# Six granules instead of nine read part of their channels before the last stores of the first stage

## The chip, the cores and the metric

The kernel runs on one core of a Trainium2 chip. The metric is the device time of one execution in microseconds (us); of several executions the median is given. The profile comes from one more execution, which has a time of its own.

## What is computed

The input x is (16, 128, 64, 64) in float32: 16 images, 128 channels, 64 rows, 64 columns. The reference, cut to what matters:

```
def _gn(v, G=32, eps=1e-05):            # normalise over 4 channels x 64 x 64
    ...
x = x + _L0_conv_ref(_gn(x), L0_conv_weight)       # depthwise 5x5, padding 2
x = x + _L1_conv_ref(_gn(x), L1_conv_rota_matrix)  # einsum('hvc,bchw->bvhw', R, feats)
```

The second part mixes all 128 channels of a pixel with a matrix that depends on the row h. It can begin only when all 128 channels of the first sum (x1 below) and the statistics of all 32 channel groups are known.

## The kernel before, in words

**First stage.** The 32 groups of 4 channels are taken one after the other. A group is 1 MB: 128 partitions (2 halves of 8 images, times 64 rows), with 4 channels, 8 images and 64 columns in each. Its loads come from x in pieces of 256 bytes. TensorE does the convolution as matmuls over the rows (line 661), ScalarE and VectorE add the input (lines 426, 543, 546), and `store` (lines 243 to 247) writes the group to a scratch tensor in DRAM, `x1_dram`, laid out channel first. Groups 0 to 25 are stored from ScalarE's queue, groups 26 to 31 (`SYNC_STORES = 26`) from SyncE's queue (SP). The last group is stored in two halves of two channels, 512 KB each. The statistics of x1 are measured as the groups go by; those of the last 8 groups are picked by a small matmul (line 726) and kept by VectorE (line 616), after which the second stage may normalise.

**Second stage.** x1 is read back with the channels on the partitions. A granule is 4 rows of 8 images: 128 channels with 2048 floats each, 1 MB, in runs of 8 KB. There are 32 granules (`GRANULES`) and 11 buffers for them (`IRING`). ScalarE and GpSimd normalise a granule (lines 471 and 394; VectorE helps with the first, line 622), TensorE multiplies each of its rows with that row's matrix (line 771, preceded by the transposed matrices of line 720), VectorE adds x1 (line 632), and each pair of granules is stored to `out` as one DMA of 2 MB (line 309). The results of a pair stand in one of three buffers (`ORING = 3`).

**The order on SP's queue.** SP issues, in the order of its program, the loads of the first stage, the stores of groups 26 to 31, and everything of the second stage. The change touches what stands between these stores. In the step of the first stage with number 29 (`AHEAD_STEP`), when 28 groups are safely in DRAM (`AHEAD_GROUPS`), SP begins to load the first 112 channels of some granules ahead of the stores of groups 28 to 31 (`load_granule`, lines 274 to 278). When the last store has landed, the remaining 16 channels of each of them follow, 128 KB each; below they are called the tails. Then come the granules that were not begun, whole. The few lines that say this:

```
for n in AHEAD.get(s, ()):
    load_granule(n, slice(0, AHEAD_GROUPS * GC))
...
store(sp, GROUPS - 1, slice(0, 2))
store(sp, GROUPS - 1, slice(2, GC))
groups_stored(sp, GROUPS)
for n in range(EARLY):
    load_granule(n, slice(AHEAD_GROUPS * GC, C))
...
for n in range(EARLY, IRING):
    load_granule(n, slice(0, C))
```

The granules from number 11 on are each loaded when granule n - 11 has been added (SP waits for `out_ready`), and SP's wait for a granule's end stands before the store of its pair and before the next load.

Of the kernel before, what the change touches and what calls it, by code (L numbers as in the profile page):

```python
# [54 lines left out]
SLOT_ORDER = (7, 8, 9, 10, 4, 5, 6, 0, 1, 2, 3)  # L55
AHEAD_GROUPS = 28
AHEAD_STEP = AHEAD_GROUPS + 1
AHEAD = {AHEAD_STEP: range(0, 5), AHEAD_STEP + 1: range(5, 7), AHEAD_STEP + 2: range(7, 9)}
EARLY = 9
SYNC_STORES = 26  # L60
ORING = 3
TURNED = 4
# [9 lines left out]
def conv_rotate_kernel(nc, x, weight, rota, out):  # L72
# [4 lines left out]
    with ExitStack() as ctx:  # L77
# [137 lines left out]
        def granule_landings(n):  # L215
            return 16 * (n // IRING + 1) + (16 if n % IRING < EARLY else 0)

# [31 lines left out]
        def groups_stored(queue, groups):  # L249
            for k in range(YRING):  # L250
                queue.wait_ge(x1_stored[k], 16 * len(range(k, groups, YRING))
                              + (16 if groups == GROUPS and k == (GROUPS - 1) % YRING else 0))
# [7 lines left out]
        def _(sp):  # L260
# [13 lines left out]
            def load_granule(n, channels):  # L274
                u, half = unit_half(n)
                sp.dma_start(tin[n % IRING][channels].rearrange("p h j w -> p (h j w)"),
                             x1_dram[channels, half, u * RH:(u + 1) * RH].rearrange("c h j w -> c (h j w)")
                             ).then_inc(in_landed[n % IRING], 16)

            for s in range(GROUPS + 1):  # L280
# [12 lines left out]
                if s == AHEAD_STEP:  # L293
                    sp.wait_ge(norm2_stored, 32 * (LAST // NBATCH))
                    sp.dma_start(norm2[0:LAST * GC], norm2_dram[0:LAST * GC]).then_inc(norm2_landed, 16)
                    groups_stored(sp, AHEAD_GROUPS)
                for n in AHEAD.get(s, ()):
                    load_granule(n, slice(0, AHEAD_GROUPS * GC))
# [3 lines left out]
# [3 lines that stand above are left out]
# [8 lines left out]

            for n in range(EARLY, IRING):
                load_granule(n, slice(0, C))
# [484 lines left out]
```

## Time and profile before

| | |
|---|---|
| median of 3 runs | 476.41 us (476.32 to 477.0) |
| time of the profiled execution | 472.46 us |
| its span | 470.7 us |
| TensorE busy (matmul) | 414.4 us, 88% |
| VectorE, ScalarE, GpSimd busy | 359.1 us (76%), 275.4 us (59%), 232.1 us (49%) |
| moved by DMA | 139.03 MB, mean 295 GB/s |
| chain that ended last, TensorE and DMA | 65% and 24% of the span |

Times in the trace count from the start of the span. In rows of the timeline the first number is the start, the second the time until the last of the merged instructions ended; a DMA issue is the time of the instruction on the queue, not that of the transfer. The time from an issue to the landing of its data is told by the DMA view alone.

### The profile page before, as it was taken

The page shows a single profiled execution, that of the slowest core. Times are in us where ns is not written, and L with a number is a line of the kernel's source. Part 1 is how long each engine was busy: PE and PEld are TensorE (multiplying, and loading weights), DVE is VectorE, ACT ScalarE, POOL GpSimd, SP SyncE. Part 2 cuts the span into 40 slices and gives each one's busy share as a digit, 9 for nine tenths or more (in the row PEclk, how much of TensorE's full clock was granted, in tenths as well). Part 3 has the DMA queues.
Part 4 walks back from the last instruction along what each step waited for, and adds up shares of the span by engine and source line. Part 5 has one row for each costly group of instructions (what it writes and reads, how often), then busy time and mean ns, then how long its engine had stood idle before and what let it go on. Part 6 is the DMA issues. An engine that isn't in the chain of part 4 may idle for free.

```text
span 470.7 us, 8916 instructions
## 1 busy us (share of the span) xinstructions
PE 414.4 (88%) x3235; PEld 219.6 (47%) x3235; DVE 359.1 (76%) x726; ACT 275.4 (59%) x538; POOL 232.1 (49%) x300
## 2 busy tenths in 40 slices
PE   5888999999999999999999999717999977787791
PEld 5444455555555555555555555413444433333340
DVE  6679999999999999998999975815776544445581
ACT  4164757676675675675676766305777655474560
POOL 5456667665675675665766651003444432242330
PEclk9799999999999999999999999857999999899997
DMA  9989999999989999999999289979999999999997
GB/s 175 198 190 242 262 247 263 260 225 241 318 227 310 259 270 286 241 299 278 251 263 256 110 268 325 313 255 158 416 418 414 411 414 414 419 419 415 407 408 268
DMA packets 177139, 139.03 MB, mean 295 GB/s; under 512 B 137160, under 2 KB 139208, under 8 KB 173000
## 3 DMA queue, kind: packets, MB, share of 16 engines
q1 hardware_dynamic: 159000, 110.15, 80.4%
q10 hardware_dynamic: 18096, 28.32, 17.7%
q8 instruction: 26, 0.43, 0.4%
q14 instruction: 17, 0.14, 0.1%
HBM read 71.32 MB, written 67.12 MB: 294 GB/s over the span
## 4 chain that ended last, share of the span: by engine, by line
PE 65%; DMA 24%; DVE 7%; issue 1%; ACT 1%; ACTq 0%; SPq 0%; DVEq 0%
PE ps L661 55%; DMA out_dram<-area 19%; PE ps L771 8%; DMA x_scratch<-area 3%; DVE area L632 2%; DVE stats L554 2%; DMA area<-in_x_dram 1%; DMA area<-x_scratch 1%; DVE area L546 1%; DVE stats L561 1%; DVE dev L601 1%; PE ps L679 0%; PE ps L671 0%; DVE area L622 0%; ACT area L449 0%
## 5 line engine op out<-in xcount | busy, mean ns | idle before, releaser
L661 PE MATMUL ps<-area 64*64 64x496 f32 (+2 forms) x2560 | 280.6, 589 | 4.2 <-ACT area L449 1.7
L661 PEld LDWEIGHTS ps<-area 64*64 64x64 f32 x2560 | 144.7, 134 | 94.8 <-issue 93.3
L352 POOL TENSOR_TENSOR area<-mask,area 128x325 f32<-128x325 f32 x128 | 130.9, 1046 | 68.5 <-PE ps L661 47.4
L771 PE MATMUL ps<-area 128*128 128x512 f32 x256 | 117.7, 609 | 30.2 <-DVE area L632 17.7
L632 DVE TENSOR_TENSOR area<-ps,area 128x512 f32<-128x512 f32 x128 | 82.2, 686 | 57.9 <-DMA out_dram<-area 39.9
L471 ACT ACTIVATE area<-area,norm 128x256 f32<-128x256 f32 x157 | 80.6, 588 | 61.1 <-PE ps L771 49.8
L449 ACT ACTIVATE area<-area,affine 128x256 f32<-128x256 f32 x189 | 96.4, 588 | 30.1 <-DVE affine L578 30.1
L394 POOL TENSOR_SCALAR area<-area,norm 128x256 f32<-128x256 f32 x95 | 51.7, 557 | 116.8 <-PE ps L771 84.6
L426 ACT ACTIVATE area<-ps 64x512 f32<-64x512 f32 x128 | 75.7, 592 | 47.4 <-PE ps L661 44.9
L771 PEld LDWEIGHTS ps<-area 128*128 128x128 f32 x256 | 48.0, 195 | 89.1 <-issue 56.3
L554 DVE BATCH_NORM_STATS2 stats<-area 128x6 f32<-128x512 f32 x128 | 80.4, 692 | 4.2 <-DMA area<-in_x_dram 4.2
L561 DVE BATCH_NORM_STATS2 stats<-area 128x6 f32<-128x512 f32 x128 | 80.9, 695 | 1.1
L367 POOL TENSOR_SCALAR area<-area,affine 128x256 f32<-128x256 f32 x64 | 47.9, 759 | 36.3 <-DVE affine L578 36.3
L546 DVE TENSOR_TENSOR area<-area 128x512 f32<-128x512 f32 x64 | 44.0, 687 | 0.5 <-ACT area L426 0.5
L543 DVE TENSOR_TENSOR area<-ps,area 128x512 f32<-128x512 f32 x64 | 43.7, 682 | 0.7 <-PE ps L661 0.7
L444 ACT ACTIVATE std<-ps,eps 128x16 f32<-128x16 f32 (+1 forms) x36 | 9.8, 272 | 35.9 <-PE ps L671 35.9
L679 PEld LDWEIGHTS ps<-stats,half_mean 64*64 64x64 f32 x144 | 18.7, 137 | 25.0 <-issue 19.0
L671 PEld LDWEIGHTS ps<-spread,half_mean 64*64 64x64 f32 x144 | 18.2, 136 | 19.0 <-issue 16.2
L679 PE MATMUL ps<-stats,half_mean 64*64 64x16 f32 (+1 forms) x144 | 16.7, 196 | 5.6 <-DVE affine L578 3.1
L576 DVE RECIPROCAL affine<-std 128x16 f32<-128x16 f32 (+1 forms) x36 | 8.5, 236 | 15.0 <-ACT std L444 15.0
L671 PE MATMUL ps<-spread,half_mean 64*64 64x16 f32 (+1 forms) x144 | 16.3, 194 | 1.7 <-DVE spread L603 1.7
L720 PEld LDWEIGHTS ps<-ident,rot_all 128*128 128x128 f32 x64 | 7.9, 141 | 7.4 <-issue 6.7
(38 smaller groups left out, 80.4 us busy)
## 6 DMA issues: line engine op xcount, KB each, us to landing
area<-in_x_dram SPq DMA_DIRECT2D x248, 128.0 KB, 4.3
out_dram<-area SPq DMA_DIRECT2D x15, 2048.0 KB, 17.7
x_scratch<-area ACTq DMA_DIRECT2D x26, 1024.0 KB, 5.7
area<-x_scratch SPq DMA_DIRECT2D x23, 1024.0 KB, 14.9
area<-x_scratch SPq DMA_DIRECT2D x9, 896.0 KB, 17.7
x_scratch<-area SPq DMA_DIRECT2D x5, 1024.0 KB, 17.7
out_dram<-area SPq DMA_DIRECT2D x2, 1024.0 KB, 9.4
area<-x_scratch SPq DMA_DIRECT2D x9, 128.0 KB, 6.5
```

What stands on the lines that cost most here:

```text
L352: last = nc.gpsimd.tensor_tensor(taps[k % TRING][:, c * KW:(c + 1) * KW].rearrange("p d (b r) -> p d b r", r=TAPS), bass.AP(tensor=of_rows ...
L367: last = nc.gpsimd.tensor_scalar(normed[k % GRING][:, :, j], xin[k % XRING][:, j], affine[:, k, 0, 0, j:j + 1], affine[:, k, 0, 1, j:j + 1 ...
L394: last = nc.gpsimd.tensor_scalar(gn[n % NRING][:, :, j], tin[n % IRING][:, :, j], norm2[:, unit_half(n)[1], 0, j:j + 1], norm2[:, unit_hal ...
L426: last = nc.scalar.activation(y[k % YRING][rows, 2 * pair + 1], ps[half, bank + 1].rearrange("p (j w) -> p j w", j=J), ACT.Identity)
L449: last = nc.scalar.activation(normed[k % GRING][:, :, j], xin[k % XRING][:, j], ACT.Identity, scale=affine[:, k, 0, 0, j:j + 1], bias=affi ...
L471: last = nc.scalar.activation(gn[n % NRING][:, :, j], tin[n % IRING][:, :, j], ACT.Identity, scale=norm2[:, unit_half(n)[1], 0, j:j + 1], ...
L546: nc.vector.tensor_tensor(y[k % YRING][:, c + 1], y[k % YRING][:, c + 1], xin[k % XRING][:, :, c + 1], ALU.add).then_inc(x1_ready, 1)
L554: last = nc.vector.bn_stats(out=stats[:, k % 2, 0, 2 * q:2 * q + 2].rearrange("p j f -> p (j f)"), in_=xin[k % XRING][:, 2 * q:2 * q + 2]. ...
L561: last = nc.vector.bn_stats(out=stats[:, (k + 4) % 2, 1, 2 * q:2 * q + 2].rearrange("p j f -> p (j f)"), in_=y[k % YRING][:, :, 2 * q:2 * ...
L632: nc.vector.tensor_tensor(tout[slot][:, :, rows + h], ps[:, (n * RH + h) % 6, :].rearrange("p (j w) -> p j w", j=J), tin[n % IRING][:, h], ...
L661: last = nc.tensor.matmul(ps[half, bank + c].rearrange("p (j w) -> p j w", j=J)[:, :, outs], taps[k % TRING][rows, (2 * pair + c) * KW + d ...
L771: nc.tensor.matmul(ps[:, m % 6, :], rot_t[u % TURNED][:, h], gn[n % NRING][:, h], start=True, stop=True).then_inc(rotated, 1)
```

## The change

`EARLY`, the number of granules that are begun ahead, goes from 9 to 6. In the three steps that issue them they were five, two and two; now they are three, two and one.

```diff
-AHEAD = {AHEAD_STEP: range(0, 5), AHEAD_STEP + 1: range(5, 7), AHEAD_STEP + 2: range(7, 9)}
-EARLY = 9
+AHEAD = {AHEAD_STEP: range(0, 3), AHEAD_STEP + 1: range(3, 5), AHEAD_STEP + 2: range(5, 6)}
+EARLY = 6
```

`EARLY` also enters `granule_landings`, so that readers of the granules 6, 7 and 8 now wait for one DMA instead of two; nothing is computed otherwise than before.

SP's queue at the end of the first stage, as a difference (before -, changed +). L246 is a store of x1 (128 partitions x 4 channels x 512), L295 a small read of the statistics, L276 the load of a granule, here its first 112 channels:

```order
 L246 DMA x_scratch<-area 128x4x512 x2
 L295 DMA norm<-norm_scratch 96x32
-L276 DMA area<-x_scratch 112x2048 x5
+L276 DMA area<-x_scratch 112x2048 x3
 L246 DMA x_scratch<-area 128x4x512
 L276 DMA area<-x_scratch 112x2048 x2
 L246 DMA x_scratch<-area 128x4x512
-L276 DMA area<-x_scratch 112x2048 x2
+L276 DMA area<-x_scratch 112x2048
 L246 DMA x_scratch<-area 128x4x512
 L246 DMA x_scratch<-area 128x2x512 x2
```

Two loads fewer stand ahead of the store of group 28, and one fewer ahead of the store of group 30.

SP's queue at the start of the second stage, right behind those rows. L276 is now a tail (16 channels) or a whole granule (128), L309 the store of a pair of granules:

```order
-L276 DMA area<-x_scratch 16x2048 x9
-L276 DMA area<-x_scratch 128x2048 x3
+L276 DMA area<-x_scratch 16x2048 x6
+L276 DMA area<-x_scratch 128x2048 x6
 L309 DMA out_dram<-area 128x8x512
 L276 DMA area<-x_scratch 128x2048 x2
```

Three tails have gone and three whole granules have come, ahead of the first store of the output. The last of the whole granules in these rows is number 11, the first that waits for a buffer.

## Rows read from the trace of the kernel before

**Rows 1.** The page: DMA share and rate in 40 slices of 11.8 us

```profile
DMA  9989999999989999999999289979999999999997
GB/s 175 198 190 242 262 247 263 260 225 241 318 227 310 259 270 286 241 299 278 251 263 256 110 268 325 313 255 158 416 418 414 411 414 414 419 419 415 407 408 268
```

**Rows 2.** Chain that ended last, around the change of stage: start, us, what

```profile
299.94 0.59 ACT area L426
...
301.18 0.70 DVE area L546
301.90 13.51 DMA x_scratch<-area
315.48 3.38 DMA area<-x_scratch
318.96 2.04 DVE area L622 x4
...
345.44 16.92 DMA out_dram<-area
```

**Rows 3.** Timeline of SP's queue, 265 to 345 us: issues

```profile
273.57 2.38 SPq L276 DMA_DIRECT2D area<-x_scratch  x5
277.81 0.38 SPq L246 DMA_DIRECT2D x_scratch<-area  x1
278.23 0.97 SPq L276 DMA_DIRECT2D area<-x_scratch  x2
286.47 0.38 SPq L246 DMA_DIRECT2D x_scratch<-area  x1
286.89 4.33 SPq L276 DMA_DIRECT2D area<-x_scratch  x2
295.06 7.20 SPq L246 DMA_DIRECT2D x_scratch<-area  x3
315.48 11.80 SPq L276 DMA_DIRECT2D area<-x_scratch  x12
330.83 0.39 SPq L309 DMA_DIRECT2D out_dram<-area  x1
...
338.14 0.39 SPq L309 DMA_DIRECT2D out_dram<-area  x1
```

**Rows 4.** Stretches: window, length, busy time by engine, PEclk, DMA share, GB/s

```profile
277.00:290.00 13.00, 13.00 (x137) 7.27 (x132) 10.02 (x24) 9.51 (x19) 4.71 (x6) 1.00 1.01 288
...
303.50:308.30 4.80, 1.64 (x17) 1.29 (x16) 3.49 (x11) 0.53 (x2) 0.00 (x0) 0.50 0.98 250
309.00:312.50 3.50, 0.00 (x0) 0.00 (x0) 0.12 (x1) 0.00 (x0) 0.00 (x0) 0.50 1.04 404
316.50:326.50 10.00, 5.41 (x13) 2.64 (x14) 4.36 (x8) 3.85 (x8) 3.02 (x6) 0.63 1.05 123
328.00:330.80 2.80, 2.80 (x11) 1.36 (x10) 2.30 (x4) 1.97 (x5) 0.55 (x3) 1.00 1.02 424
331.00:460.00 129.00, 111.26 (x287) 49.59 (x285) 75.75 (x119) 79.79 (x157) 46.40 (x86) 0.99 1.03 414
```

**Rows 5.** DMA view, the one store issued at 269.16: KB, us to landing

```profile
x_scratch<-area SPq DMA_DIRECT2D x1, 1024.0 KB, 4.3
```

**Rows 6.** Line 276, 315.4 to 319.5 us: issue min/median/max ns, first and last; landings

```profile
L276 SPq DMA_DIRECT2D area<-x_scratch x9: 320/420/421, 315.5 to 319.1; - x9
...
DMA to landing us min/median/max: 3.4/6.5/9.0
```

**Rows 7.** DMA view, line 276, issues near 319.55, at 320.01, at 326.96

```profile
area<-x_scratch SPq DMA_DIRECT2D x1, 1024.0 KB, 10.9
...
area<-x_scratch SPq DMA_DIRECT2D x1, 1024.0 KB, 13.2
...
area<-x_scratch SPq DMA_DIRECT2D x1, 1024.0 KB, 8.7
```

**Rows 8.** Timeline of the engines, 308 to 327 us

```profile
308.74 0.39 DVE L616 COPY norm<-ps 32x16 f32<-32x16 f32 x2 [0.56 <-PE ps L726]
...
321.09 5.11 PE L771 MATMUL ps<-area 128*128 128x512 f32 x8 [12.46 <-DVE area L622]
```

**Rows 9.** Waits of VectorE from 315 us on: total, times, longest

```profile
DVE area L632 <- DMA out_dram<-area: 39.9, 9, 5.7
```

## Prediction

> **What bounds the kernel now.** I first read the slices of the page. The DMA engines are busy nearly throughout, but what they move differs: about 250 GB/s in the first stage, 158 in the slice around the change of stage (317 to 329 us), and 407 to 419 from there until the last slice [rows 1]. So the second stage is bound by transfers at a steady rate: 414 GB/s from 331 to 460 us with the engines' share at 1.03, and VectorE waits nine times, 39.9 us in all, for an output store to free its buffer [rows 4, 9]. TensorE is busy there too, but it isn't what the end waits for. What remains after the change of stage is a fixed list of megabytes, and the end comes when the list is done.
>
> Next I read the chain that ended last. It shows a hole: the last half of group 31 is ready and its store issued at 301.90 us, but it lands 13.51 us later, at 315.41. Only then may the tails be read, and the first lands 3.38 us on [rows 2]. The queue shows why the store took so long: nine loads of 112 channels and the stores of groups 28 to 31 were issued on the same queue from 273.57 us on [rows 3], and the last store stands behind them all. A store of 1 MB with little ahead of it landed in 4.3 us [rows 5]. So the last store waits mostly for the backlog.
>
> The third reading is of rates. While 112-channel loads are what the queue works off (277 to 290 us, and again 303.5 to 308.3), it moves 288 and 250 GB/s with the share at about 1; when the stores behind them have their turn (309 to 312.5), 404 GB/s. The tails move 123 GB/s at a share of 1.05, and the whole granules after them 424 GB/s [rows 4]. A granule that is read in two parts thus costs the DMA engines more time than one that is read whole. That is what the change works on.
>
> **The change, part by part.**
>
> *1. Three loads of 112 channels less ahead of the last stores.* Each is 896 KB, 0.917 MB. At the 288 GB/s of the stretch in which they are nearly alone that is 3.2 us. Bounds: at the 404 GB/s of the fastest stretch in this backlog, 2.3 us; at the 250 GB/s of the slowest, 3.7 us. I take 3.2, since the stretch of 13 us is the longest and holds the fewest other transfers. Three give 9.6 us (6.8 to 11.0), so the last store would land at 305.8 us. This has a floor, because the store is still issued at 301.90: TensorE, ScalarE and VectorE don't depend on these loads, and their order isn't changed. An unhindered 1 MB took 4.3 us, a half should take between that and 4.3 minus the 1.2 us that half a MB takes at 424 GB/s, so the landing can't be before 305.0, and the gain can't be above 10.4 us. The queue doesn't run dry before: three loads keep it busy from 274.8 to 284.4, the store of group 28 (2.5 us) to 286.9, two loads to 293.3, store 29 to 295.8, one load to 299.0, store 30, which is issued at 295.06, to 301.5, and the first half of group 31 to 302.8. It would be nearly empty when the last half comes, which is as it should be. **Gain 9.6, between 6.8 and 10.4.**
>
> *2. Three tails less.* The nine tails were issued from 315.5 to 319.1. The first landed after 3.4 us, at 318.9; the ninth, issued near 319.15, after 9.0, at 328.15 [rows 6]. Eight intervals in 9.3 us: 1.16 us each, though a tail is only 128 KB. Three less are **3.5 us gained**; 3 x 131 KB at 123 GB/s gives 3.2 as the lower end.
>
> *3. Three whole granules more.* They are read after the tails, in the stretch that bounds the end. The issues near 319.55, at 320.01 and at 326.96 landed at 330.45, 333.2 and 335.65 [rows 7], and the ninth tail at 328.15: three granules in 7.5 us, 2.5 each (2.3 to 2.75), as 1.049 MB at 424 GB/s also gives. Nothing hides them. **Cost 7.5, between 6.9 and 8.2.**
>
> The Trainium skill (DMA: Bandwidth & Descriptors, Anatomy of one DMA) puts each transfer at about 2.0 us plus its bytes at 436 GB/s, which is measured there for transfers issued by GpSimd. By it a load of 112 channels is 4.1 us, a tail 2.3 and a whole granule 4.4, and the sum would be -12.3 - 6.9 + 13.2 = -6.0 us. The rows show the price of queued transfers to be 1.16 and 2.5 us, so here the fixed part lies beside the next transfer, and I keep to the rows.
>
> *4. The engines.* The normalisation needs the kept statistics, ready at 309.13 us [rows 8], and the first tail, which would now land at 305.8 + 3.4 = 309.2. Both come together, so the first matmul, which stood 5.6 us behind the first tail's issue (321.09 against 315.48), comes at about 311.4, 9.7 us earlier. This costs nothing as long as the DMA engines have work meanwhile. After the last tail (landing near 315.0) they have granules 6 to 10, five times 2.5 us, to 327.5, and granule 11, whose buffer was free 5.9 us after the first matmul (326.96 against 321.09 [rows 7, 8]) and so now at 317.3, to 330. The first output store was issued 9.7 us after the first matmul and so comes at 321.1. That leaves 9 us of cover; if the engines started later than that, each further us would be lost.
>
> *5. Moved waits.* SP has the same waits as before. It issues less in steps 29 and 31, so no store is issued later. The three granules that now come whole land at about 317.5, 320 and 322.5, and are wanted later: a pair of granules takes the engines 7.3 us (330.83 to 338.14 between the first two output stores [rows 3]), so that after the first pair at 321.1 and two more they come to number 6 at 335.7.
>
> **Sum:** -9.6 - 3.5 + 7.5 = **-5.6 us**. With all the bounds one way, -10.4 - 3.5 + 6.9 = -7.0 and -6.8 - 3.2 + 8.2 = -1.8. The profiled execution would go from 472.46 to 466.9 us (span 470.7 to 465.1). It lay 3.95 us below the median of the runs; the difference carries over, so the median goes from 476.41 to 470.8.
>
> **Rivals.**
>
> *A. The last store isn't waiting for the backlog (slower).* If the loads of 112 channels only filled time that the DMA engines had to spare, say because the stores of group 30 and 31 have their own long way to DRAM, then taking them away wins nothing at the hole. What is left is -3.5 + 7.5 = +4.0 us, 480.4. It decides against the change when the last store lands later than 315.4 - 4.0 = 311.4. For it speaks that the queue's share is near 1 at every rate, which doesn't tell work from waiting [rows 4]. Against it speak the 4.3 us of a store with little ahead of it, and that the engines compute nothing from 309.13 to 318.96 while the queue works [rows 2, 8], so that nothing of theirs can hold the store. The Trainium skill (DMA: Bandwidth & Descriptors, Rules for kernel authors) advises to issue a DMA early and to wait on it late so that it overlaps computing; the change does the opposite for 2.75 MB. Chance 0.10.
>
> *B. The chain moves as a whole (faster still).* In the chain, what follows the hole is computing up to 345.44 us [rows 2]. Were the second stage bound by its engines, the end would come earlier by the whole 9.7 us, and the time would be 466.7. Against it: 414 GB/s with the engines' share at 1.03 without a break, and VectorE waiting for stores. Chance 0.05.
>
> *C. The gain is lost in the second stage (no change).* Six whole granules in a row now stand before the first output store. Its landing, and with it the buffer for the fourth pair, would come late, VectorE and SP behind it stop, and if the queue ran dry, 5.6 us of holes would eat the gain: 476.4. Against it: a 2 MB store issued at 345.44 already landed after 16.92 us [rows 2], and the queue was full. Chance 0.05.
>
> **How the numbers follow.** The forecast has 0.80. A measurement of this kernel can tell about 0.2% (1 us) from no change. The forecast's own spread is from -1.8 to -7.0, all of it faster; with B that is 0.85. C is the same, 0.05, and A slower, 0.10. The range takes the forecast's bounds with 0.2 us more on the fast side and 0.1 less on the slow side, about the spread of the runs: 469.2 to 474.5. It leaves out A, B and C, together 0.20.
>
> **What would show it.** Right: six loads of 112 channels and six tails; the last store landing in 3 to 5 us, at 305 to 307; the first tail issued right after, the tails 1.16 us apart; the first matmul at about 311.4; 410 to 420 GB/s from about 317 to the end; first output store near 321; VectorE's waits for output stores longer than 39.9 us. Wrong: a last store landing after 308 (term 1 too large), after 311 (rival A); slices under 400 GB/s between 317 and 350 us (rival C); an end that moves by more than 7 us (rival B).

## The result and the profile after

| | before | with the change |
|---|---|---|
| median | 476.37 us (474.52 to 477.0, 4 runs) | 469.0 us (468.57 to 469.48, 4 runs) |
| time of the profiled execution | 472.46 us | 469.4 us |
| its span | 470.7 us | 467.5 us |

The ratio is 0.9863, with a 95% interval of 0.9831 to 0.9895: 6.5 us faster, which from 476.37 us leads to 469.8. The forecast was 5.6 us and 470.8 us (469.2 to 474.5). The ratio puts the time inside that range; the plain median, 469.0, lies 0.2 us below it. The two profiled executions differ by only 3.2 us of span; why, the experiments show.

The page with the change: rate in 40 slices, now of 11.7 us, beside [rows 1].

```profile
DMA  9989999998989999999999469979999999999998
GB/s 175 198 180 248 267 253 253 273 230 233 320 225 281 283 247 305 258 256 248 285 248 282 144 189 314 324 168 377 415 414 411 414 413 417 417 419 417 409 403 283
```

The poor slice lies one place earlier (304 to 316 us, 168), and its neighbour already has 377 where before it was 158. The chain that ended last, beside [rows 2]:

```profile
302.81 5.97 DMA x_scratch<-area
308.86 3.21 DMA area<-x_scratch
312.17 2.04 DVE area L622 x4
```

The last store lands in 5.97 us instead of 13.51. It is issued 0.9 us later than in the other execution. In the traces below (spread_tails aside) it is issued anywhere from 301.1 to 303.7 us, in no order by the number of early loads, so this is put down to scatter. SP's queue, beside [rows 3]:

```profile
275.58 1.26 SPq L276 DMA_DIRECT2D area<-x_scratch  x3
278.72 0.38 SPq L246 DMA_DIRECT2D x_scratch<-area  x1
279.14 0.98 SPq L276 DMA_DIRECT2D area<-x_scratch  x2
287.38 0.38 SPq L246 DMA_DIRECT2D x_scratch<-area  x1
287.80 0.51 SPq L276 DMA_DIRECT2D area<-x_scratch  x1
295.97 7.20 SPq L246 DMA_DIRECT2D x_scratch<-area  x3
308.86 13.07 SPq L276 DMA_DIRECT2D area<-x_scratch  x12
325.49 0.39 SPq L309 DMA_DIRECT2D out_dram<-area  x1
```

Three, two and one load are ahead, as planned, and the tails are issued as soon as the last store has landed. Stretches (columns as in [rows 4]):

```profile
280.00:288.00 8.00, 8.00 (x86) 4.51 (x80) 5.12 (x13) 5.04 (x11) 2.62 (x4) 1.00 0.99 290
303.00:306.00 3.00, 1.42 (x20) 1.28 (x20) 2.30 (x7) 0.59 (x2) 0.00 (x0) 1.00 1.03 399
306.00:308.80 2.80, 1.16 (x10) 0.94 (x10) 1.64 (x8) 0.27 (x1) 0.00 (x0) 0.58 0.28 109
312.00:316.00 4.00, 1.70 (x2) 0.84 (x3) 2.03 (x4) 3.65 (x7) 2.90 (x5) 0.50 1.03 109
321.00:329.00 8.00, 8.00 (x25) 3.90 (x24) 5.79 (x9) 6.35 (x13) 3.47 (x7) 1.00 1.01 421
335.00:450.00 115.00, 100.19 (x250) 44.63 (x249) 62.20 (x101) 69.88 (x137) 40.64 (x75) 0.94 1.03 415
```

The kinds of transfer have nearly the same rates as before: 290 GB/s while loads of 112 channels have their turn, 399 for the stores behind them, 109 for tails, 421 and 415 for the second stage. (The 123 GB/s of [rows 4] for the tails are of a stretch that reaches past them; before, from 319 to 326 us, it was 110.) The third row shows how the queue drains: in the last 2.8 us before the store lands, the mean share of the DMA engines is only 0.28. That isn't new, though [rows 4] has no stretch of it. The last 2.8 us before the landing in the kernel before:

```profile
312.60:315.40 2.80, 0.00 (x0) 0.00 (x0) 0.00 (x0) 0.00 (x0) 0.00 (x0) 0.50 0.34 130
```

So a slow end of nearly 3 us belongs to both holes. That some of the 16 engines are done sooner and the store waits for the slowest would explain it; the share is a mean over the engines and doesn't show that. Line 276 from 308.8 to 311.3 us, the six tails, beside [rows 6]:

```profile
L276 SPq DMA_DIRECT2D area<-x_scratch x6: 320/420/422, 308.9 to 311.1; - x6
...
DMA to landing us min/median/max: 3.2/5.2/6.6
```

From 312.1 to 317.7 for five intervals is 1.13 us each. VectorE's waits for output stores, beside [rows 9]:

```profile
DVE area L632 <- DMA out_dram<-area: 34.5, 8, 5.6
```

### The profile page after: what moved, and what is told of

The parts are those of the page before. It is cut to its first block, busy times and chain, and to the rows that moved or that the text cites. A ratio compares the mean times of both kernels' runs of the same rounds, so it can differ in the third digit from the quotient of the medians.

```text
span 467.5 us, 8913 instructions
## 1 busy us (share of the span) xinstructions
PE 421.1 (90%) x3235; PEld 222.2 (48%) x3235; DVE 358.2 (77%) x726; ACT 275.3 (59%) x538; POOL 232.1 (50%) x300
## 4 chain that ended last, share of the span: by engine, by line
PE 56%; DMA 23%; DVE 8%; SPq 7%; issue 1%; ACT 1%; ACTq 0%; DVEq 0%
PE ps L661 46%; DMA out_dram<-area 19%; PE ps L771 9%; SPq L230 7%; DVE stats L554 3%; DVE area L632 3%; DMA area<-in_x_dram 2%; DMA x_scratch<-area 1%; DVE area L546 1%; DMA area<-x_scratch 1%; DVE stats L561 1%; DVE dev L601 1%; PE ps L679 0%; DVE area L622 0%; PE ps L671 0%
## 5 line engine op out<-in xcount | busy, mean ns | idle before, releaser
L771 PE MATMUL ps<-area 128*128 128x512 f32 x256 | 123.6, 634 | 19.6 <-DVE area L632 14.8
L632 DVE TENSOR_TENSOR area<-ps,area 128x512 f32<-128x512 f32 x128 | 81.7, 686 | 62.3 <-DMA out_dram<-area 34.5
L771 PEld LDWEIGHTS ps<-area 128*128 128x128 f32 x256 | 49.4, 201 | 80.1 <-issue 50.1
L720 PEld LDWEIGHTS ps<-ident,rot_all 128*128 128x128 f32 x64 | 9.1, 158 | 10.0 <-issue 9.3
```

The source lines that it names most:

```text
L632: nc.vector.tensor_tensor(tout[slot][:, :, rows + h], ps[:, (n * RH + h) % 6, :].rearrange("p (j w) -> p j w", j=J), tin[n % IRING][:, h], ...
L771: nc.tensor.matmul(ps[:, m % 6, :], rot_t[u % TURNED][:, h], gn[n % NRING][:, h], start=True, stop=True).then_inc(rotated, 1)
```

## The experiments

Two lengths are read from each profile: the **hole**, from the issue of the last store to that of the first tail, and the **rest**, from there to the end of the span. They come from the issues of the store (line 246, its last start), those of line 276, and the span. Each ratio is taken against executions of the kernel before from the same rounds, whose medians ran from 473.99 to 476.37 us; so kernels of different rounds are compared by their ratios.

| kernel | begun ahead | hole | rest | median, us | ratio to before (95%) |
|---|---|---|---|---|---|
| before | 5, 2, 2 | 13.6 | 155.2 | 476.37 | 1 |
| before_again | 5, 2, 2 | 15.9 | 155.3 | 475.5 | 1.0006 (0.998 to 1.0032) |
| tails_in_two | 5, 2, 2 | 15.0 | 155.2 | 475.54 | 1.0015 (0.999 to 1.004) |
| early7_520 | 5, 2 | 10.1 | 158.0 | 471.34 | 0.9929 (0.9901 to 0.9957) |
| the change | 3, 2, 1 | 6.1 | 158.6 | 469.0 | 0.9863 (0.9831 to 0.9895) |
| change_again | 3, 2, 1 | 4.9 | 159.2 | 467.73 | 0.9855 (0.9834 to 0.9876) |
| early6_510 | 5, 1 | 6.4 | 159.1 | 469.45 | 0.9879 (0.9853 to 0.9906) |
| early5_320 | 3, 2 | 3.3 | 160.3 | 467.04 | 0.9838 (0.9811 to 0.9865) |
| interleave5 | 3, 2 | 3.3 | 160.6 | 467.21 | 0.9846 (0.9814 to 0.9878) |
| early4_220 | 2, 2 | 2.8 | 161.5 | 467.82 | 0.9866 (0.9841 to 0.9891) |
| early3 | 3 | 2.8 | 162.8 | 470.26 | 0.9906 (0.9878 to 0.9934) |
| late_split | 3, 2, 1 | 5.3 | 163.5 | 472.05 | 0.9935 (0.9914 to 0.9957) |

**before_again**, the kernel before, unchanged.

> The kernel before once more, for the scatter of its time and of its profile. The profiled execution of before was 3.95 us below the median of its runs, that of the change agrees with its runs. If the offset belongs to the profiled execution alone, this profile lies near 476.4 like the runs; if executions of this kernel scatter between 472 and 477, the profiles of the two differ in one stretch, which the stretches of time show. Ratio to before 1.000.

Its profiled execution took 475.65 us, near its median. Its chain has the difference:

```profile
302.66 15.78 DMA x_scratch<-area
318.52 3.25 DMA area<-x_scratch
```

Span 473.8 against 470.7: the hole is 2.3 us longer, the last store is issued 0.8 us later, the rest is the same to 0.1 us. With tails_in_two, shape112 (16.3 us, where stage one is the same too) and the first profile, four executions with nine granules ahead have holes of 13.6, 15.9, 15.0 and 16.3, mean 15.2. The profile on which the forecast rests had the shortest of them. So executions of the kernel before do scatter (471.89 to 476.44 here), and a part of it lies in the hole. What the unprofiled runs spent where can't be seen.

The traces show where this scatter of the hole comes from. The first early load is issued when 28 groups have landed, and so right behind the landing of the store of group 27. In the first profile that store landed in 4.3 us [rows 5], here in 5.7. The early loads began 28.3 us ahead of the issue of the last store in the one and 26.9 in the other, where the same backlog reached further past it. Of the seven other executions with six, seven or nine granules, change_again is like the first profile (4.3 and 28.3 us); the rest have 5.4 to 5.9 us and 26.7 to 27.2. Why that store lands sooner in two of them is open. The steadier length is that of the backlog, from the issue of the first early load to the landing of the last store:

| granules ahead | executions | first early load to last landing, us |
|---|---|---|
| nine | before, before_again, tails_in_two, shape112 | 41.8, 42.7, 42.0, 43.2; mean 42.5 |
| seven | early7_520 | 36.8 |
| six | the change, change_again, early6_510, late_split | 33.2, 33.2, 33.0, 32.4; mean 32.9 |

Three loads are 9.5 us of it, 3.2 each. (The one profile with seven splits this unevenly: 5.6 us for two loads, 3.9 for the third.)

**late_split**, the position of three loads without their saving. Behind the tails:

```diff
-            for n in range(EARLY, IRING):
+            for n in range(EARLY, SPLIT):
+                load_granule(n, slice(0, AHEAD_GROUPS * GC))
+                load_granule(n, slice(AHEAD_GROUPS * GC, C))
+            for n in range(SPLIT, IRING):
                 load_granule(n, slice(0, C))
```

with `SPLIT = 9`, also in `granule_landings`.

> As the change, but granules 6, 7 and 8 are still read in two parts, both parts behind the tails. Theory 1 (a granule in two parts costs the DMA engines 3.2 + 1.16 us instead of 2.5, wherever it is read): the last store lands in about 6 us as with the change, and the second stage starts with 3 x 1.9 = 5.6 us more work, so the time is 5.6 us above the change and near that of before. Theory 2 (what counts is only that the last stores land earlier): the time of the change, 7 us below before.

472.05 us, and its interval is apart from that of the change. Theory 2 falls: the hole is as short as with the change (5.25 us of chain), but the rest is 4.5 us longer than the mean of the three kernels with six granules (159.0). A granule in two parts costs 1.5 us more than a whole one behind the stores, where theory 1 had 1.9. It isn't quite the time of before either: 0.9935. By holes and rests it stands 15.2 - 5.3 = 9.9 against 163.5 - 155.2 = 8.3. So moving the three loads is worth something by itself, 1.6 us by these stretches and 3.1 by the ratio, where theory 1 gave nearly nothing; that they aren't split is worth the rest. Why a split costs 0.4 us less here than theory 1 had is open.

**early3**, `AHEAD = {AHEAD_STEP: range(0, 3)}`, `EARLY = 3`.

> Three granules begun ahead, all in the first of the steps. Theory 1: the last store can land at most 1.7 us earlier than with the change (4.3 us after its issue instead of 6), three tails less give 3.5, three whole granules more cost 7.5, so the time is 2.3 to 4 us above the change, still below before. Theory 2 (fewer ahead is better throughout): not above the change.

470.26 us: below before, and by the ratios (0.9906 and 0.9863) above the change, though these two intervals overlap a little. The DMA engines had run out of work before the last half came (stretches, columns as above; it was issued at 301.9):

```profile
299.00:300.00 1.00, 1.00 (x15) 0.55 (x8) 0.26 (x2) 0.03 (x1) 0.00 (x0) 1.00 0.00 0
302.00:303.00 1.00, 0.64 (x8) 0.62 (x9) 0.34 (x3) 0.45 (x1) 0.00 (x0) 0.91 0.19 74
303.00:304.00 1.00, 1.00 (x11) 0.96 (x10) 0.93 (x5) 0.00 (x0) 0.00 (x0) 0.50 1.01 383
304.00:305.00 1.00, 0.38 (x5) 0.29 (x4) 1.00 (x3) 0.27 (x1) 0.00 (x0) 0.50 0.19 68
```

So 2.8 us is the floor of the hole (four granules have it too), and a granule that is taken from the early ones there only costs. "Fewer is better throughout" falls: the interval of the ratio with three (0.9878 to 0.9934) lies wholly above that with five (0.9811 to 0.9865).

**early4_220, early5_320, early6_510, early7_520**: other numbers and places of the early loads; the diff is that of `AHEAD` and `EARLY` alone, for instance

```diff
-AHEAD = {AHEAD_STEP: range(0, 5), AHEAD_STEP + 1: range(5, 7), AHEAD_STEP + 2: range(7, 9)}
-EARLY = 9
+AHEAD = {AHEAD_STEP: range(0, 3), AHEAD_STEP + 1: range(3, 5)}
+EARLY = 5
```

> Seven granules begun ahead, five and two. Theory Q: the last store lands 3.2 us later than with the change, at 9.2 us after its issue, and one granule less read whole gives 1.3 back: 1.9 us above the change, 470.9. Rival L: with no such load in the third step the store lands as with the change, and the time is 1.3 us below it.

> Six granules begun ahead as with the change, but five in the first step, one in the second and none in the third. Theory Q (sum of the backlog): the queue is never dry either way, so the last store lands after the same 6 us and the time is that of the change within 1 us. Rival L (the load that stands right before the stores of groups 30 and 31 holds them): last store in 4 us or less, 2 us below the change.

> Five granules begun ahead, three and two. Theory Q (the last store waits for the sum of the backlog, 3.2 us for each load of 112 channels, and no less than the 2.8 us that it took with three granules): it lands 2.8 to 3.5 us after its issue instead of 6.0, 2.5 to 3.1 us earlier, and one granule read whole instead of in two parts, behind the last store, costs 1.3: 1.2 to 1.8 us below the change, about 467.5. Rival: the 6.0 us with the change is not backlog but slow draining, and stays: 1.3 us above the change, 470.3.

> Four granules begun ahead, two and two. Theory Q: the last store can't land much earlier than with five (3.2 us after its issue; 2.8 with three), and one granule more that is read whole behind it costs 1.3: 0.9 us above five, 467.9, below the change. Rival (fewer is better as long as any backlog is left): below 467.0.

The chains of the first two, early7_520 first:

```profile
303.67 10.05 DMA x_scratch<-area
313.79 3.22 DMA area<-x_scratch
```

```profile
301.86 6.27 DMA x_scratch<-area
308.21 3.18 DMA area<-x_scratch
```

With seven it was 10.05 us, where 9.2 were expected; with six in the order five and one, 6.27 us where the change has 5.97: the backlog counts, not which load stands last, and rival L falls on both (471.34 us with seven, slower than the change, ratios 0.9929 and 0.9863, intervals apart; 469.45 with five and one, where it gave 2 us below the change). With five the hole is 3.3, with four 2.8 us. Theory Q gave 467.5 and 467.9; measured were 467.04 and 467.82. The rest grows from 155.2 with nine to 162.8 with three, 1.27 us a granule. With five the DMA engines are busy without a break up to the issue of the last half; with four they aren't. Early5_320 first, then early4_220:

```profile
295.00:302.00 7.00, 5.97 (x64) 3.54 (x54) 5.62 (x12) 3.21 (x7) 0.00 (x0) 1.00 1.01 378
```

```profile
299.00:301.00 2.00, 2.00 (x24) 1.26 (x16) 1.26 (x3) 0.28 (x1) 0.00 (x0) 1.00 0.34 129
```

**interleave5**, five granules ahead; behind each tail but the first comes a whole granule (beside early5_320).

```diff
                 load_granule(n, slice(AHEAD_GROUPS * GC, C))
+                if n:
+                    load_granule(EARLY + n - 1, slice(0, C))
...
-            for n in range(EARLY, IRING):
+            for n in range(2 * EARLY - 1, IRING):
```

> Five granules begun ahead, and behind the last store each tail but the first is followed by a whole granule, instead of all tails and then the whole ones. Theory I (during a tail most of the way into the buffers is idle, and engines that are done with their row go on with the next transfer, so that tails hide beside whole granules): up to 4 x 0.85 = 3.4 us below five granules in the plain order, 463.6. Rival (every one of the 16 DMA engines is held by its own row of the tail): no difference to 467.0 within 1 us.

467.21 against 467.04 us, rest 160.6 against 160.3: nothing gained. From 306 to 324 us the two moved (interleave5, then early5_320):

```profile
306.00:324.00 18.00, 14.49 (x45) 7.39 (x46) 10.81 (x24) 9.95 (x21) 6.32 (x11) 0.78 1.00 307
```

```profile
306.00:324.00 18.00, 14.49 (x42) 7.21 (x43) 9.65 (x22) 9.37 (x20) 6.34 (x11) 0.70 1.01 318
```

A tail doesn't hide beside its neighbour.

**shape112**, one size changed in the steady stage; the last 16 channels of 21 granules are left out:

```diff
-                    load_granule(n + IRING, slice(0, C))
+                    load_granule(n + IRING, slice(0, AHEAD_GROUPS * GC))
```

> The kernel before, but the 21 granules of the second stage from number 11 on are read with their first 112 channels alone (this leaves out the last 16 channels of x1 in them, whose place keeps older data). They are 2.75 MB less in a stretch bound by transfers. Theory S (a transfer over 112 partitions is slow by its shape, 3.2 us against 2.5 for 128): 21 x 0.7 = 15 us slower. Theory N (the 288 GB/s before the change of stage come from what runs beside these loads): 2.75 MB at 414 GB/s, 6.6 us faster.

486.2 us, ratio 1.0252 (1.0204 to 1.0301), though 2.75 MB less are moved. The same stretch of before and of shape112:

```profile
345.00:440.00 95.00, 79.74 (x210) 35.71 (x209) 50.57 (x81) 58.93 (x116) 34.01 (x63) 0.98 1.03 415
```

```profile
345.00:440.00 95.00, 78.37 (x190) 35.04 (x189) 47.12 (x75) 53.20 (x106) 31.10 (x57) 0.91 1.03 341
```

The share is 1.03 in both, the rate falls from 415 to 341. A pair of granules is a store of 2.10 MB and two loads; 3.93 MB at 341 GB/s are 11.5 us, less 5.05 for the store (at 415) leaves 3.2 us a load, just the price taken for term 1. By the rest, 166.8 against 155.2, it is 0.55 us more for each of 21 loads, so 3.05. Theory N falls. The low rate of the early loads comes with their shape, 112 rows into 112 partitions, and not with what ran beside them.

**tails_in_two**, twice the number of tails, each half the size:

```diff
             for n in range(EARLY):
-                load_granule(n, slice(AHEAD_GROUPS * GC, C))
+                for rows in (slice(0, 2), slice(2, RH)):
+                    load_granule(n, slice(AHEAD_GROUPS * GC, C), rows)
```

> The kernel before, but each tail is read as two DMAs of two rows each, 64 KB, so 18 tails of half the size. Theory F (a tail costs 1.16 us because a short transfer has a fixed part): the tails take near twice the time, 10.4 us more before granule 9, and the time is up to 10 us above before. Theory P (a transfer over 16 partitions moves at 115 GB/s by its shape): the same bytes take the same time, no difference to before beyond 1 us.

`load_granule` takes the rows here, and `granule_landings` counts one landing more. No difference (1.0015, 0.999 to 1.004), and the rest is 155.2 as before. A fixed part of about 1 us per tail would have shown as 10 us. Theory F falls.

**spread_tails**, one execution, for the rate of tails that write other partitions (the diff is cut: `load_granule` also takes the partitions, and four buffers are zeroed first; the last 16 channels stand in wrong places):

```diff
+                sp.wait_ge(in_landed[n], 16)
-                load_granule(n, slice(AHEAD_GROUPS * GC, C))
+                load_granule(n, slice(AHEAD_GROUPS * GC, C), slice(7, P, 8))
```

> The change, but the 16 rows of a tail are written to partitions 7, 15, ... 127 instead of 112 to 127 (this puts the last 16 channels in the wrong places; four buffers are zeroed at the start, and SP waits for the first part of a granule before its tail). Theory P (a tail is slow by which partitions it writes): the six tails land closer together than 1.16 us, some 0.6 us. Rival (a tail is slow because each DMA engine has but one row of it): 1.16 us apart as before.

Line 276 from 313.7 to 317.3 us, and the rate from 315.3 to 318.3, while only tails are under way (the first whole granule is issued near 317.5):

```profile
L276 SPq DMA_DIRECT2D area<-x_scratch x6: 542/587/588, 313.8 to 316.9; - x6
...
DMA to landing us min/median/max: 2.7/2.9/3.0
```

```profile
315.30:318.30 3.00, 0.00 (x0) 0.00 (x0) 1.90 (x5) 1.72 (x4) 1.64 (x3) 0.50 0.67 197
```

Each tail lands about 2.9 us after its issue, whether first or last, so the spacing is that of the issues, 0.6 us, and the DMA engines are busy only 0.67 of the time. The same 128 KB in the same 16 rows go at 197 GB/s at least, instead of 109. Which partitions are written decides; how fast such tails could go if they were issued faster isn't shown. The time of this execution, 473.06 us, isn't compared: its first stage is longer, with the last store issued only at 308.3 us.

The Trainium skill (SBUF — State Buffer, Door 1: The DMA port swizzle) tells which of 16 ports a partition belongs to: by its table 112 to 127 reach 4 ports, and 7, 15, ... 127 reach 8, for which it gives about 109 and 218 GB/s. The trace of the change agrees with the first, 109; the 197 of this one is above what it gives for 4 ports and doesn't test the 218.

**change_again**, the kernel with the change once more.

> The kernel with the change once more, for its scatter and to set it beside five and four granules. If the times of the other runs carry over, the median is 469.0, and five granules ahead (467.04) are faster by 2 us; Theory Q puts that difference at 1.2 to 1.8. If the 469.0 of the first measurement was high or the 467.04 low, the two come within 1 us of each other, and five is no better than six.

467.73 us, ratio 0.9855, and a hole of 4.85 us:

```profile
301.57 4.85 DMA x_scratch<-area
306.50 3.13 DMA area<-x_scratch
```

Its span is 465.7 us. Beside 467.04 us with five granules (0.9838, 0.9811 to 0.9865) the intervals overlap widely. That five beats six isn't shown. Both, six in the order three, two, one, beat nine and seven with intervals that lie apart; three (0.9878 to 0.9934) lies apart from five and just apart from change_again, but not from the first measurement of six.

## Why the prediction was right, point by point

- **What bounds it.** Right: the second stage moves 415 GB/s with the change (335 to 450 us) and 414 without (331 to 460), and the rest grew with the work that was added. The first matmul came 6.8 us earlier and the end of the profiled execution only 3.2, so computing earlier moved nothing by itself (rival B).
- **Term 1, the hole, 9.6 us.** The mean hole is 15.2 us over four executions with nine granules and 5.7 over four with six (the change, change_again, early6_510, late_split): 9.5. The mechanism is shown twice over, by seven, five and four granules and by the floor of 2.8 us, which I had set at 3.1. By the lengths of the backlog it is 9.5 as well. Against the one execution that I worked from, the step was too good: the landing came at 308.8 instead of 305.8, later than the 308 that I had named as a sign of term 1 too large, and it took 5.97 us instead of 3 to 5. Of the 3.0 us, 2.0 are a later start of the backlog, 275.58 instead of 273.57, which I had left where it was; the other 1.0 is its length, 33.2 against 41.8 us, 8.6 less and not 9.6. The price of a load isn't refuted by that: in change_again, where the backlog begins at 273.25, the store lands in 4.85 us, at 306.4, inside the 305 to 307 of the forecast.
- **From the profile to the median.** I let the 3.95 us between the profiled execution and the median carry over. They didn't: with the change the profiled execution is at 469.4 and the median at 469.0. The first profile was an execution with an early start of the backlog and so a short hole; that, the later issue of the store and a rest that grew by 3.4 are why the spans differ by 3.2 us and not by 5.6. The forecast for the median starts from the median, and its terms are priced by rates, so it didn't hang on where that execution lay.
- **Terms 2 and 3, -3.5 + 7.5 = +4.0.** Measured 159.0 - 155.2 = +3.8. A tail is 1.13 us (1.16 forecast), and the 2.5 us of a whole granule stand in 421 GB/s. The Trainium skill (DMA: Bandwidth & Descriptors, Anatomy of one DMA) gives each transfer that GpSimd issues a fixed 2.0 us. It isn't in the price of the queued ones here, which SP issues: tails_in_two has nine transfers more and takes no more time.
- **The sum.** By the means, -9.5 + 3.8 = -5.7 us; the ratios give -6.5 and -6.9. What is left is less than the scatter of the kernel before, and no trace shows where it lies. The medians themselves differ by 7.4 us, more than the 7 that I had named as a sign of rival B; the growth of the rest speaks against it.
- **Step 4, the engines.** Wrong in size, without effect. The first matmul came at 314.30 instead of 311.4, since the first tail landed at 312.07; the first output store at 325.49 instead of 321.1. The cover held: 421 GB/s from 321 to 329.
- **Waits for output stores.** I expected more than 39.9 us, and they fell to 34.5. Why was not looked into; the rate of the second stage shows that nothing hangs on it.
- **Rival A** (slower, 480.4) needed a landing after 311.4. The hole shrank by 9.5 us. The advice of the Trainium skill (DMA: Bandwidth & Descriptors, Rules for kernel authors) to issue early holds here only up to five or six granules: further early loads stand in the same queue ahead of what all else waits for. **Rival C** fell with the rates from 321 us on; the slice with 377 GB/s, from 315.6 to 327.2 us, still has the last tails in it (the last lands at 317.7). That the early loads were worth something is shown at the other end: with three, the time rises again.

## What to carry to other kernels

Prefetching on the queue that carries the last stores before a change of stage cost twice here: the stores waited for it, and a transfer cut into parts by partitions cost the DMA engines more time than a whole one. Prefetch as much as keeps the queue busy until the last store is issued and no more; here that is five or six granules (with four, at 467.82 us, not clearly worse), where nine were begun. Price a transfer by the rate of its own shape in a stretch where it is nearly alone, and look whether the share near 1 moves 110, 290 or 420 GB/s.

## What the runs showed that I hadn't expected

- Loads of 128 partitions move at 421 GB/s, of 112 at 290 (3.2 us for seven eighths of the bytes that take 2.5), of 16 neighbouring ones at 109, and of 16 spread ones at 197 or more, all with rows of 8 KB. Why 112 is so slow was not tried apart, so it stays open.
- The hole with nine granules ahead varied from 13.6 to 16.3 us between executions of the same order of work, that with six from 4.9 to 6.4. About half of the first spread comes from when the backlog could begin, 26.9 to 28.3 us before the last store's issue, and half from its length, 41.8 to 43.2 us.
- TensorE's granted clock was at 0.50 (1.2 GHz) from 310 to 320 us, though it had begun to work at 314.30:

```profile
310.00:320.00 10.00, 5.70 (x7) 2.53 (x8) 3.62 (x7) 3.65 (x7) 2.90 (x5) 0.50 1.00 206
...
319.30:322.00 2.70, 2.70 (x10) 1.30 (x9) 1.38 (x2) 1.04 (x3) 0.96 (x2) 0.85 1.01 422
```

Before, it rose at 324 (worked out from the mean of 0.63 in [rows 4]), 3 us after the first matmul at 321.09; with the change it rose near 320 (from 0.85 above), 6 us after. The first eight matmuls took 6.56 instead of 5.11 us [rows 8]. It cost nothing that the traces show: the DMA engines moved 421 GB/s from 321 us on.
